# Sorted experts: weights as the stationary operand, loaded from HBM for each tile, and the score multiplied in before the scatter

## The reference

```python
logits = x @ gate_w                              # [tokens, 8 experts]
top_val = jnp.max(logits, axis=-1, keepdims=True)
top_id = jnp.argmax(logits, axis=-1)
score = jax.nn.sigmoid(top_val)
xs = x * score
g = jnp.einsum('th,ehi->eti', xs, rt_gate)       # h 128, i 256
u = jnp.einsum('th,ehi->eti', xs, rt_up)
act = jax.nn.silu(g) * u
y = jnp.einsum('eti,eih->eth', act, rt_down)
routed = jnp.einsum('eth,te->th', y, onehot)     # each token takes its own expert
shared = _swiglu(x, sh_gate, sh_up, sh_down)     # added for every token
```

## Time and profile before

| | before |
|---|---|
| median of 3 runs | 600.24 us |
| lowest, highest | 598.56, 604.52 us |
| the profiled execution | 596.14 us |
| its span, first to last instruction | 593.7 us |
| mean granted TensorE clock | 0.954 |
| PE busy in the span | 516.4 us (87%) |
| DVE, ACT, POOL busy | 411.6, 310.4, 274.4 us |
| sorted experts, first rows issued to last result kept | 311.4 to 408.7 us |

### The profile page before, as it was taken

One profiled execution on the slowest core, in us unless ns is written; L12 is line 12 of the kernel. 1 busy time (PEld: TensorE's weight loads), 2 busy tenths in 40 slices (PEclk: granted clock), 3 DMA queues, 4 the chain that ended last, 5 costly groups with the idle time before them and its releaser, 6 DMA issues. The chain is left out here.

```text
span 593.7 us, 19118 instructions
## 1 busy us (share of the span) xinstructions
PE 516.4 (87%) x5902; PEld 365.0 (61%) x5903; DVE 411.6 (69%) x1348; ACT 310.4 (52%) x843; POOL 274.4 (46%) x693
## 2 busy tenths in 40 slices
PE   1789999999999999987927699997676789999998
PEld 0456666666666666654523355554444579999997
DVE  3888888898988888833374344542445589999974
ACT  2477777777777777652313456652333244444420
POOL 5545544465556555554320100006542588887520
PEclk9899999999999999988966899997989889999999
DMA  7900120000000000000011612221000001111000
GB/s 269 378 16 21 35 122 4 3 12 12 10 9 9 9 10 9 12 17 13 19 54 32 126 44 63 68 69 39 25 9 6 9 26 39 36 36 31 19 19 27
DMA packets 24215, 26.24 MB, mean 44 GB/s; under 512 B 4969, under 2 KB 21153, under 8 KB 23521
## 3 DMA queue, kind: packets, MB, share of 16 engines
q1 hardware_dynamic: 20688, 15.31, 8.4%
q0 software_dynamic: 3472, 10.26, 5.9%
HBM read 17.50 MB, written 7.91 MB: 43 GB/s over the span
## 5 line engine op out<-in xcount | busy, mean ns | idle before, releaser
L892 DVE TENSOR_REDUCE negm<-PS 128x4 f16<-128x512 f32 x128 | 84.7, 684 | 1.0 <-PE PS L1236 0.8
L651 ACT ACTIVATE pexp<-PS 128x512 f32<-128x512 f32 x128 | 78.3, 619 | 9.1 <-PE PS L1249 9.1
L1548 PE MATMUL PS<-w,vp 128*128 128x128 f32 x512 | 63.1, 277 | 0.0
L1548 PEld LDWEIGHTS PS<-w,vp 128*128 128x128 f32 x512 | 60.3, 193 | 0.1
L1236 PE MATMUL PS<-ktp,arena 128*64 128x128 f16 x1024 | 53.2, 227 | 4.7 <-DVE negm L892 3.5
L1263 PE MATMUL PS<-pexp,vp 128*32 128x64 f32 x2048 | 54.5, 227 | 2.1 <-ACT pexp L651 0.8
L1099 DVE SCALAR_TENSOR_TENSOR pexp<-PS,xs,oS 128x256 f32<-128x256 f32 x40 | 19.4, 484 | 50.5 <-ACT oS L752 47.5
L1449 PE MATMUL PS<-rgu,xsT 128*128 x80 | 48.4, 689 | 4.4 <-ACT xsT L757 2.6
L1236 PEld LDWEIGHTS PS<-ktp,arena 128*64 128x64 f16 x1024 | 33.0, 110 | 26.3 <-issue 15.0
L1263 PEld LDWEIGHTS PS<-pexp,vp 128*32 128x32 f32 x2048 | 34.8, 110 | 22.1 <-issue 11.7
L484 POOL TENSOR_TENSOR ve<-mv,epsc 128x1 f32<-128x1 f32 x32 | 6.1, 192 | 90.3 <-DVE mv L928 90.3
(11 more groups left out here) (225 smaller groups left out, 1317.5 us busy)
## 6 DMA issues: line engine op xcount, KB each, us to landing
xs<-sorted_x SPq DMA_DIRECT2D x40, 64.5 KB, 1.8
sorted_y<-YS SPq DMA_DIRECT2D x40, 64.0 KB, 1.6
arena<-mT SPq DMA_DIRECT2D x128, 1.0 KB
rgu<-in_rt_gate_up_dram POOLq DMA_DIRECT2D x1, 2048.0 KB, 8.0
out_dram<-X SPq DMA_DIRECT2D x32, 64.0 KB, 1.6
X<-in_x_dram SPq DMA_DIRECT2D x1, 1536.0 KB, 8.5
CK<-in_ctx_k_dram SPq DMA_DIRECT2D x1, 1536.0 KB, 11.7
CV<-in_ctx_v_swapped_dram SPq DMA_DIRECT2D x1, 1536.0 KB, 15.8
```

Source lines behind the costliest of these rows:

```text
L651: nc.scalar.activation(pexp[:, j, :], PS[:, 2 + j % 2, :], ACT.Exp).then_inc(S["exped"], 1)
L892: dve.tensor_reduce(negm[:, a.par, :, j], PS[:, j % 2, :].rearrange("p (h k) -> p h k", h=HG), AX.X, ALU.max, negate=True).then_inc(S["max ...
L1548: nc.tensor.matmul(PS[:, 6 + y.par, 0:D], z[:, y.par, e, :], w1[:, e * D:e * D + D], start=(e == 0), stop=False)
```

## The change

The lift is turned round. For each sorted tile SyncE now loads, besides the 128 rows, the 128 x 512 gate and up weights of the tile's expert from HBM (256 KB) into one of four slots of `wst`, and TensorE uses them as the stationary operand: four matmuls of 128 columns whose output is the activation already transposed. So the two transposes of the activation, their copy on ScalarE, and the 2 MB `rgu` with its load go, VectorE's product writes `act2T` directly, and the step is one stage shorter. The score is multiplied into the rows by GpSimd before the scatter, so silu and the product have none. Row number and expert of two steps are packed in one number by VectorE, and SyncE reads it once in two steps and splits it with register operations. The loads of a tile are released by the lift of the tile four back, not by its product.

```diff
-    DW = D + 1
+    ROW_STEP = 512
...
-        VALL = sb("VALL", [P, NT * DW])
+        VALL = sb("VALL", [P, NT * D])
...
-        XN2 = VALL.rearrange("p (t d) -> p t d", d=DW)
+        XN2 = VALL.rearrange("p (t d) -> p t d", d=D)
+        score = sb("score", [P, TURN])
...
-        rows_of = sb("rows_of", [P, NS], I32)
+        stepf = sb("stepf", [P, NS])
+        steps = sb("steps", [P, NS // 2], I32)
...
-        rgu = sb("rgu", [P, E * 2 * FF])
+        wst = sb("wst", [P, 4, 2 * FF])
...
-        sorted_x = nc.dram_tensor("sorted_x", (ROWS, DW), F32).ap()
+        sorted_x = nc.dram_tensor("sorted_x", (ROWS, D), F32).ap()
...
+            two_steps, expert_of, row_of = (sp.alloc_register(n) for n in ("two_steps", "expert_of", "row_of"))
+
             def load_and_store(stage):
-                l, d = stage(0), stage(7)
+                l, d = stage(0), stage(6)
                 if l:
                     if not (l.turn is None and l.n < 4):
-                        sp.wait_ge(S["e_acted"], l.freed(back=4))
-                    row = sp.value_load(rows_of[0:1, ds(l.t, 1)], min_val=0, max_val=ROWS - P)
+                        sp.wait_ge(S["e_lifted"], l.freed(back=4))
+                    if l.par == 0:
+                        sp.reg_mov(two_steps, sp.value_load(steps[0:1, ds(l.pair, 1)], min_val=0, max_val=ROW_STEP ** 2 * E ** 2 - 1))
+                    both = sp.snap(two_steps, min_val=0, max_val=ROW_STEP ** 2 * E ** 2 - 1)
+                    one = both // (ROW_STEP * E) if l.par else both % (ROW_STEP * E)
+                    sp.reg_mov(expert_of, one // ROW_STEP)
+                    sp.reg_mov(row_of, one % ROW_STEP * P)
+                    expert = sp.snap(expert_of, min_val=0, max_val=E - 1)
+                    row = sp.snap(row_of, min_val=0, max_val=ROWS - P)
+                    sp.dma_start(wst[:, l.slot, :], rt_gate_up[:, ds(expert * (2 * FF), 2 * FF)]).then_inc(wst_in[l.slot], 16)
                     sp.dma_start(xs[:, l.slot, :], sorted_x[ds(row, P)]).then_inc(xs_in[l.slot], 16)
                 if d:
                     sp.wait_ge(S["e_kept"], d.done())
                     sp.dma_start(sorted_y[ds(d.t * P, P)], YS[:, d.slot, :]).then_inc(stored[d.slot], 16)
 
-            walk(sp, NS, 7, load_and_store)
+            walk(sp, NS, 6, load_and_store)
...
-                          *((binB4[:, q * D:q * D + D], b_in) for q in range(CT)), (rgu, rt_gate_up))
+                          *((binB4[:, q * D:q * D + D], b_in) for q in range(CT)))
...
-                    pool.tensor_scalar(XN2[:, 4 * k.quad:4 * k.quad + 4, D], faded[:], 0.5, 0.5, ALU.mult, ALU.add)\
+                    rows = XN2[:, 4 * k.quad:4 * k.quad + 4, :]
+                    pool.tensor_scalar(score[:], faded[:], 0.5, 0.5, ALU.mult, ALU.add).then_inc(S["k_score"], 1)
+                    pool.wait_ge(S["r_kept"], k.done())
+                    pool.wait_ge(S["k_score"], k.quad_done(2, 0))
+                    pool.tensor_tensor(rows, rows, score[:].unsqueeze(2).to_broadcast([P, TURN, D]), ALU.mult)\
                         .then_inc(S["k_score"], 1)
...
                     pool.wait_ge(S["k_placed"], o.quad_done(2, 1))
-                    pool.wait_ge(S["k_score"], o.quad_done())
-                    pool.wait_ge(S["r_kept"], o.done())
+                    pool.wait_ge(S["k_score"], o.quad_done(2, 1))
...
-                l, f, s, a = stage(0), stage(2), stage(3), stage(4)
+                l, f, s = stage(0), stage(2), stage(3)
                 if s:
                     act.wait_ge(S["e_acted"], s.freed())
                     act.wait_ge(S["e_lifted"], s.done())
-                    nc.scalar.activation(sg[:, s.par, 0:FF], PS[:, 2 + s.par, 0:FF], ACT.Silu,
-                                         scale=xs[:, s.slot, D:DW]).then_inc(S["e_gated"], 1)
+                    nc.scalar.activation(sg[:, s.par, 0:FF], PS[:, 2 + s.par, 0:FF], ACT.Silu).then_inc(S["e_gated"], 1)
                 if f:
                     act.wait_ge(S["e_lifted"], f.freed())
                     act.wait_ge(S["e_turned"], f.done())
                     nc.scalar.copy(xsT[:, f.par, :], PS[:, f.par, 0:P]).then_inc(S["e_turned_kept"], 1)
-                if a:
-                    act.wait_ge(S["e_down"], a.freed())
-                    act.wait_ge(S["e_act_turned"], a.done())
-                    nc.scalar.copy(act2T[:, a.par, :], PS[:, 4 + a.par, 0:FF]).then_inc(S["e_act_kept"], 1)
...
-            dve.tensor_tensor(rows_of[:], rowf[:], tile_start, ALU.add).then_inc(rows_known, 1)
+            dve.tensor_tensor(stepf[:], rowf[:], tile_start, ALU.add)
             then(dve.tensor_reduce(texpf[:], tcmp[:, :, 0:E - 1], AX.X, ALU.add))
+            then(dve.scalar_tensor_tensor(out=stepf[:], in0=texpf[:], scalar=float(ROW_STEP * P), in1=stepf[:],
+                                          op0=ALU.mult, op1=ALU.add))
+            pairs_of = stepf[:].rearrange("p (s k) -> p s k", k=2)
+            then(dve.scalar_tensor_tensor(out=pairs_of[:, :, 0], in0=pairs_of[:, :, 1], scalar=float(ROW_STEP * E),
+                                          in1=pairs_of[:, :, 0], op0=ALU.mult, op1=ALU.add))
+            dve.tensor_scalar(steps[:], pairs_of[:, :, 0], 1.0 / P, None, ALU.mult).then_inc(rows_known, 1)
...
-                l, s, d = stage(0), stage(3), stage(6)
+                l, s, d = stage(0), stage(3), stage(5)
...
-                    dve.wait_ge(S["e_act_turned"], s.freed())
+                    dve.wait_ge(S["e_down"], s.freed())
                     dve.wait_ge(S["e_gated"], s.done())
-                    dve.scalar_tensor_tensor(out=hact[:, s.par, 0, 0:FF], in0=PS[:, 2 + s.par, FF:2 * FF],
-                                             scalar=xs[:, s.slot, D:DW], in1=sg[:, s.par, 0:FF],
-                                             op0=ALU.mult, op1=ALU.mult).then_inc(S["e_acted"], 1)
+                    dve.tensor_tensor(act2T[:, s.par, :], PS[:, 2 + s.par, FF:2 * FF], sg[:, s.par, 0:FF], ALU.mult)\
+                        .then_inc(S["e_acted"], 1)
...
-                f, s, a, b = (stage(i) for i in range(2, 6))
+                f, s, b = (stage(i) for i in range(2, 5))
                 if s:
-                    e_lift = pe.snap(expert_of[s.slot], min_val=0, max_val=E - 1)
                     pe.wait_ge(S["e_acted"], s.freed())
+                    pe.wait_ge(wst_in[s.slot], 16 * (s.quad + 1))
                     pe.wait_ge(S["e_turned_kept"], s.done())
-                    nc.tensor.matmul(PS[:, 2 + s.par, :], xsT[:, s.par, :], rgu[:, ds(e_lift * (2 * FF), 2 * FF)],
-                                     start=True, stop=True).then_inc(S["e_lifted"], 1)
+                    for i in range(4):
+                        last = nc.tensor.matmul(PS[:, 2 + s.par, i * P:i * P + P], wst[:, s.slot, i * P:i * P + P],
+                                                xsT[:, s.par, :], start=True, stop=True)
+                    last.then_inc(S["e_lifted"], 1)
...
-                    pe.wait_ge(S["e_act_kept"], b.done())
+                    pe.wait_ge(S["e_acted"], b.done())
...
-                if a:
-                    pe.wait_ge(S["e_act_kept"], a.freed())
-                    pe.wait_ge(S["e_acted"], a.done())
-                    for i in range(2):
-                        last = nc.tensor.transpose(PS[:, 4 + a.par, i * P:i * P + P],
-                                                   hact[:, a.par, 0, i * P:i * P + P], identf)
-                    last.then_inc(S["e_act_turned"], 1)
-
-            walk(pe, NS, 7, sorted_step)
+
```

More of the change, by code:

```diff
@@ L213, in flamingo_gated_two_layers @@
         squares = pexp
-        hact = pexp.rearrange("p (c i) t -> p c i t", c=2)
-        zeros = sb("zeros", [P, SPARE * DW])
-        xs = sb("xs", [P, 4, DW])
+        zeros = sb("zeros", [P, SPARE * D])
+        xs = sb("xs", [P, 4, D])
         xsT = sb("xsT", [P, 2, P])
@@ L353, in flamingo_gated_two_layers @@
         xs_in = [sem(f"xs_in{c}") for c in range(4)]
-        for n in "turned turned_kept lifted gated acted act_turned act_kept down kept".split():
+        wst_in = [sem(f"wst_in{c}") for c in range(4)]
+        for n in "turned turned_kept lifted gated acted down kept".split():
             S["e_" + n] = sem("e_" + n)
@@ L459, in _ @@
                    ("r_kept", 1))
-            quad_credit(pool, ("k_score", 1), ("k_summed", 3))
+            quad_credit(pool, ("k_score", 2), ("k_summed", 3))
             credit(pool, *((n, 1) for n in "l_x2 l_vars l_roots l_means l_shifts l_added".split()))
@@ L709, in step @@
                     act.wait_ge(S["k_choice"], k.quad_done(5, 0))
-                    act.wait_ge(S["k_score"], k.quad_freed())
+                    act.wait_ge(S["k_score"], k.quad_freed(2, 0))
                     nc.scalar.activation(faded[:], top[:], ACT.Tanh, scale=0.5).then_inc(S["k_faded"], 1)
@@ L729, in gates_in_drain @@
                     shared_gate(1, 1)
-                    act.wait_ge(late_in, 16 * 17)
```

(9 more changed lines are left out.)

6 lines of the change are left out of this document (3 added, 3 removed).

## The result

The changed kernel takes 615.78 us (median of 4 runs, 614.25 to 618.20) where the kernel before takes 599.4 (median of 4, three of which are the runs named ahead of the prediction): ratio 1.028, 95% interval 1.023 to 1.033, 16.4 us slower. Ratios compare the undisturbed executions of both kernels, so they need not equal the quotient of two medians. Forecast were 606.0 and 597 to 613: the sign was right, the size was not. The profiled execution took 614.88 us with a span of 613.1 at a granted clock of 0.944; before it was 593.7, so the trace shows +19.4.

A forecast was written before the change was run, and what follows sets the result against it. It took the sorted experts' ring of 1.98 us as the bound, SyncE's 1.84 hidden behind it. SyncE's train of 2.3 over 22 steps gave 6.1, less 0.3 at lift 14: +5.8 on 600.24, 606.0 us, range 597 to 613.

The forecast's parts named there:

- The attention part: Attention stage, ahead of the sort: GpSimd's added score multiply was taken to cost 0, bounds 0 to +2 us.
- The ring: Sorted experts' repeating step of lift, silu and copy on TensorE and ScalarE: from 1.98 to 1.91 us a tile.
- The start: Start of the sorted experts: first rows issued later and landing behind weights, +1.0 us.
- The burst: Plugs' spread, about 331 to 340 us: weights queued ahead of rows put lift 9 at 343.9 instead of 342.00.
- SyncE's train: SyncE's three issues, fetch and splitting per sorted tile: 2.3 us a step, bounds 2.0 to 2.55, binding from lift 14.
- the fetches: SyncE's work before a step's first issue, fetching and splitting the packed number: 1.16 us in even steps, 0.60 in odd.
- The root of the norms: GpSimd's root after the sorted experts, which the next stage awaits: some 6 us later, at unchanged distance from lift 36.
- Rival 3: SyncE and DMA queue costs add up, or TensorE's clock falls: about 613 us, chance 0.13.
- Rival 1: SyncE's step is short, 2.0 us or less, and the ring of 1.91 binds: 599.4 us, chance 0.28.
- Rival 2: TensorE's stall at the plugs goes and the shorter ring pays: 591 us, chance 0.12.

The follow-up runs named there:

- score_alone: Kernel before, with only the score multiply moved to GpSimd ahead of the scatter, silu and product without score; ratio 0.998 (0.993 to 1.003).
- before_paced: Kernel before, with the plugs' spread issued as eight DMAs of 128 KB, one behind each lift of tiles 4 to 11, instead of two of 512 KB; ratio 0.994.
- sp_unrolled: Changed kernel with SyncE's walk over the 40 tiles written out in full, no loop; ratio to before 1.013, 599.4 us.
- weights_gpsimd_own_count: Changed kernel with the weights issued by GpSimd instead of SyncE and a semaphore of its own for the score multiply; ratio to before 0.999.
- best: Changed kernel with weights issued by GpSimd, the plugs' spread in eight parts between them, SyncE's walk written out, the multiply's own semaphore; ratio to before 0.982, 588.25 us.
- fifth group: Runs on one chip: best unaltered, and best and before_paced each with one empty GpSimd instruction, beside the kernel before; ratios 0.985, 0.987, 0.994.
- weights_64_bytes: Changed kernel with the weights' issue kept but cut to 64 bytes of each row, the lift using fixed weights; ratio to before 1.015, 606.0 us.
- weights_gpsimd: Changed kernel with the weights' issue moved from SyncE to GpSimd, rows and stores staying on SyncE; ratio to before 0.990.

## Why the prediction was wrong

**The attention part** (I take 0, bounds 0 to +2) was right, though the trace after shows +5.4: `score_alone` costs nothing, and the stall came and went with the group, not with the code. The traces' 19.4 less 5.4 are 14.0 for the change, an estimate, as the sort began at 298.3 to 303.5 in the traces without the stall and at 301.8 to 307.5 in those with it. The account below explains these 14.0 of the two traces, not the 16.4 of the medians or the 10 to 23 of the groups.

**The ring** of 1.91 came at 1.85 (tiles 5 to 7 and 10 to 15). A lift took 1.15 to 1.16 as forecast, a silu 0.38 against 0.37. VectorE's product took 0.42 where 0.48 stood, off the ring. **The start** came +1.2 for +1.0.

**The burst** is the first step that failed. Lift 9 was put at 343.9; it came at 350.31, which is 344.9 without the 5.4. Then I let lift 14 come at 352.5, 8.6 later, from SyncE's issues alone. Five turns of my own ring of 1.91 are 9.6; the chain that I followed was not the latest. Silu 14 was 2.1 behind (361.63 less 354.05, less 5.44), not 0.3 ahead: 2.4 us of the miss. `before_paced` shows what this stop costs the kernel before as well: 6.8 us of the stage (88.0 to 81.2), of which some 3.5 reach the time.

**SyncE's train** is the step that failed most. I had 2.36, wrote 2.3 and had 2.55 as the high end; 2.54 to 2.56 came: 56.4 us from silu 14 to 36, not 50.6, so 5.8 us of the miss. By its terms, for four steps: the issues and their gaps were 5.92 forecast (4 x 1.48) and 5.8 measured; the fetches 2 x (1.16+0.60) = 3.52 forecast and 1.85+1.32+2 x 0.59 = 4.35 measured, with the loop's edge in the 1.85. 0.53 of the 0.83 is the loop's edge. I never priced it, since the pair of issues that I read did not straddle it. The next pair in the trace of the kernel before did:

```profile
374.08 0.34 SPq L438 DMA_DIRECT2D xs<-sorted_x  x1
...
376.31 0.34 SPq L438 DMA_DIRECT2D xs<-sorted_x  x1
```

2.23 instead of 1.84, with nobody to wait for: four steps of before's train were 7.75 (2.23+3 x 1.84), 1.94 each, and under lifts 2.02 apart the slack was 0.08 where I had written 0.18. So 0.39 of the edge stood in the trace that I had; the 0.53 is what it costs in the kernel after. The rest is 0.16 in each even step: splittings and address with the turn in them. `sp_unrolled`, without loop, has the 1.15 that I had forecast as 1.16, but from rows of a loop, so that this is no proof of the sum. The reason given for going from 2.36 to 2.3, shorter gaps where waits are long met, had no row, and took 1.3 us off. 2.4+5.8 is the 8.2 between 5.8 and 14.0.

**The root of the norms** did not keep its distance from lift 36 (2.0 more), for the swap by DMA; the stages after it absorbed this, so it had no part in the end.

**The rivals.** Rival 3 (0.13) named this outcome, a train of 2.55 and 613, and that was luck. Its 2.55 came of a weights' issue of 0.57 to 0.59, which measured 0.333, and its time of 2 us for GpSimd's multiply, which costs nothing; the train reached 2.54 by the fetches instead. A clock that falls for good did not come either: it was granted at 0.86 to 1.00 in each 10 us from 370. Rival 1 needed a train under the ring; none came until an issue left SyncE. Its time, 0.8 us under before, is then near `weights_gpsimd_own_count`'s ratio of 0.999. Rival 2's two halves are both true of other kernels: the stop at the plugs can go, and the shorter ring pays, once SyncE is relieved; but here the stop grew. (Its parts add up to 9.6 and not 9; the 591 is right.) The range ended at 613 by adding ends of 5.5 and 2; the burst's own end was left out of that sum.

**What the change is worth.** Its ring is shorter: 1.83 a tile against 1.98. `best` is faster than before by 1.3 to 1.8% in three measurements. Against `before_paced`, which has the eight parts but not the change, the medians are 0.5 to 1.1% lower on the same chips; in the fifth group the intervals overlap a little. So what the rest of `best` is worth over the eight parts is clear of noise in one group of two. The change as made saved 0.13 to 0.15 a tile in the ring of TensorE and ScalarE, and paid 0.6 a tile on SyncE, whose busy time the page doesn't show.

## What to carry to other kernels

An engine that only issues DMAs has a period like any other. Before giving it one more, add up a whole turn of its loop, edge included, from the trace, and compare with the ring it feeds; hidden slack of 0.08 us doesn't carry an issue of 0.33 and its gap. If the sum is near, move an issue to an idle queue, or write that engine's loop out.

Where two traces come from different chips or moments, take a part that the change cannot touch as a control, and run the unaltered kernel again before explaining a difference: eleven traces without and seven with a stall of 1.2 us looked like a property of the code until one program had shown both.

A bulk DMA of 1 MB in front of small urgent ones stopped the kernel before for 6 us (8.45 for 1.97 at tile 9); in eight parts, one a tile, the stop was gone. In the changed kernel it shrank and did not go. A stage that is 6.8 us shorter made the time only some 3.5 us shorter, so the time must be read beside the trace.

## What the runs showed of the hardware that was not expected

- A DMA issue on SyncE takes 0.333 us and about 0.2 of gap whether the rows are 64 bytes or 2 KB (runs `weights_64_bytes` and the kernel after); on GpSimd 0.54 for 128 rows of 2 KB (`weights_gpsimd`).
- A load of 128 rows (64 KB) lands 2.8 us after their issue beside weights of 256 KB a step, and 1.8 beside weights of 8 KB (medians of 40).
- The turn of a loop on SyncE costs 0.53 us in the kernel after and 0.39 in the kernel before, of which the branch's own row shows 45 ns.
- The same program ran with ScalarE's copy 1.2 us late once in four steps in one group, and without in another; it makes four steps 0.8 us longer, 31.4 for 30.6.
